# A selective scan on VectorE: two scans of 256 columns joined into one of 512, with the carry moved into the input

## What is computed

```python
def step(h, inp):
    dt_t, Bt, Ct, xt = inp
    dA = jnp.exp(dt_t[..., None] * A)
    h = dA * h + (xt * dt_t)[..., None] * Bt[:, None, :]
    y = jnp.einsum('bdn,bn->bd', h, Ct)
    return (h, y)
h0 = jnp.zeros((B, D_INNER, D_STATE), x.dtype)
_, ys = jax.lax.scan(step, h0, inputs)
y = jnp.transpose(ys, (1, 0, 2)) + x_ssm * D_param
```

## Time and profile before

| | us |
|---|---|
| median of 3 runs | 2015.43 |
| lowest, highest | 2011.38, 2016.09 |
| the profiled execution | 2016.48 |
| its span | 2014.4 |
| mean granted TensorE clock | 0.908 of full speed |

### The profile page before, as it was taken

How to read it: one execution, slowest core, us unless ns; L and a number is a source line. 1 busy time by engine, 2 the same in 40 slices (tenths; PEclk the granted TensorE clock), 3 DMA queues, 4 the chain that set the end, 5 groups by cost and what they waited for, 6 DMA issues and landing times. The chain is left out here.

```text
span 2014.4 us, 26268 instructions
## 1 busy us (share of the span) xinstructions
PE 1643.1 (82%) x7600; PEld 1165.7 (58%) x7600; DVE 1562.5 (78%) x2994; ACT 1021.0 (51%) x2232; POOL 919.6 (46%) x722
## 2 busy tenths in 40 slices
PE   5788777887878877778567999989997999989890
PEld 3566566666666666666454554753566454753570
DVE  1899999999999999999965435882578545881478
ACT  2766777667877577776632232415233232424240
POOL 0677787777777777767751010160105210260004
PEclk8888888988889888989768999989999999999995
DMA  3301111011111011110103000001000100000000
GB/s 122 136 18 48 59 59 54 11 55 58 59 59 44 17 58 58 59 48 6 57 12 111 0 22 0 1 1 46 21 1 0 47 21 0 1 0 21 0 1 21
DMA packets 38440, 71.25 MB, mean 35 GB/s; under 512 B 3698, under 2 KB 31955, under 8 KB 33971
## 3 DMA queue, kind: packets, MB, share of 16 engines
q1 hardware_dynamic: 38290, 69.45, 10.1%
HBM read 60.79 MB, written 8.65 MB: 34 GB/s over the span
## 5 line engine op out<-in xcount | busy, mean ns | idle before, releaser
L605 POOL TENSOR_TENSOR state_c<-state,c_bc 128x1024 f32<-128x1024 f32 x256 | 603.5, 2362 | 234.4 <-DVE state L668 220.9
L668 DVE TENSOR_TENSOR_SCAN state<-decay,carry,bu_ps 128x256 f32<-128x256 f32 x768 | 527.5, 727 | 0.0
L485 ACT ACTIVATE decay<-dt_sb,negA 128x256 f32<-128x256 f32 x1024 | 433.7, 498 | 3.1 <-issue 3.1
L653 DVE TENSOR_TENSOR bu_ps<-u_sb,b_ps 128x512 f32<-128x512 f32 x512 | 344.7, 673 | 47.7 <-POOL u_sb L546 40.1
L350 PE MATMUL y_ps<-ident_sb,state_c 128*128 128x128 f32 x2048 | 304.8, 298 | 23.0 <-DVE yg L636 13.9
L350 PEld LDWEIGHTS y_ps<-ident_sb,state_c 128*128 128x128 f32 x2048 | 263.8, 155 | 54.6 <-POOL state_c L605 27.3
L1225 POOL TENSOR_TENSOR big<-big,g_sb 128x1024 f32<-128x1024 f32 x29 | 68.7, 2369 | 453.0 <-DVE big L1333 432.1
L271 PE MATMUL w_ps<-xT_sb,w_conv 128*128 128x256 f32 (+1 forms) x1024 | 236.8, 385 | 13.8 <-DVE w_conv L706 12.8
L271 PEld LDWEIGHTS w_ps<-xT_sb,w_conv 128*128 128x128 f32 x1024 | 192.8, 193 | 40.0 <-DVE w_conv L706 12.8
L946 PE MATMUL ps<-kTm,qT 128*128 128x308 f32 x512 | 140.7, 438 | 29.9 <-DVE oT L1302 25.2
L668 DVE TENSOR_TENSOR_SCAN state<-decay,bu_ps 128x256 f32<-128x256 f32 x256 | 160.2, 665 | 0.0
(11 more groups left out here) (168 smaller groups left out, 2471.3 us busy)
## 6 DMA issues: line engine op xcount, KB each, us to landing
c_bc<-c_scratch SPq DMA_DIRECT2D x32, 1024.0 KB, 5.8
res<-in_x SPq DMA_DIRECT2D x16, 256.0 KB, 2.8
x_scratch<-res SPq DMA_DIRECT2D x16, 256.0 KB, 7.4
big<-x_scratch SPq DMA_DIRECT2D x4, 1024.0 KB, 7.5
xa<-x_scratch SPq DMA_DIRECT2D x4, 1024.0 KB, 5.7
out_x<-acc SPq DMA_DIRECT2D x4, 1024.0 KB, 4.8
xT_sb<-in_xT SPq DMA_DIRECT2D x12, 259.0 KB, 3.0
w_sb<-in_w SPq DMA_DIRECT2D x2, 1024.0 KB, 13.4
```

What stands on the lines that cost most here:

```text
L485: nc.scalar.activation(decay[:, n % RING, j, :], dt_sb[:, i[1] % 2, j, :], ACT.Exp, scale=negA[:, j * NS + n:j * NS + n + 1]).then_inc(s_d ...
L605: nc.gpsimd.tensor_tensor(state_c[:, n % RING, :, :], state[:, n % RING, :, :], c_bc[:, q, n, :].unsqueeze(1).to_broadcast([P, CT, TC]), A ...
L653: nc.vector.tensor_tensor(bu_ps[m % 3][:, :].rearrange("p (j n) -> p j n", j=2), u_sb[:, i[1] % 2, 2 * h:2 * h + 2, :], b_ps[n % 2][:, 0:T ...
L668: nc.vector.tensor_tensor_scan(state[:, n % RING, j, :], decay[:, n % RING, j, :], bu_ps[m % 3][:, e * TC:(e + 1) * TC], carry[:, n, j:j + ...
```

## The change

Two scans of a half step become one scan of 512 columns that runs over both tiles. For this to be right at the seam and at the start, column 0 of every `decay` tile is 0 (a memset of POOL at the start; ACT's exponentials now write columns 1 to 255 only), and the scan's initial value is always 0.0. What the first column should have got from the chunk before enters through u*b: column 0 of `bu_ps` becomes u*b + dA*carry. For this there are new instructions, in the chunks with c != 0:

- POOL `first_arg`: dt of the first column times A, for all states and tiles, 128x64, after `make_dt` at place 11.
- ACT `first_decay`: exp of it, 128x64, behind `take_y_back` at place 15, behind all decays of the turn. (These two are made for every chunk.)
- POOL `injections`: `inject` = first_dA * carry, 128x48 for the states 0 to 11 at place 13 of the turn before, and 128x16 for the states 12 to 15 at place 4 of the chunk's own turn.
- DVE, in each `make_bu`: the product leaves out column 0 (128x510), and a SCALAR_TENSOR_TENSOR of 128x2 writes column 0 of both tiles, with `b_ps[:, 0:1]` as its scalar (a pointer into PSUM). For the first half step it waits on `s_inj`, the first `injections`.

The scans no longer wait on `s_carry`, and for one `s_decay` in place of two.

```diff
@@ PE b_row
-                pe.wait_ge(s_bu, at(i, 2 * NS, 2 * n + 2))
+                pe.wait_ge(s_bu, at(i, 4 * NS, 4 * n + 4))
@@ ACT
+            def first_decay(k):
+                act.wait_ge(s_arg, at(k, 1, 1))
+                nc.scalar.activation(first_dA[:, k[1] % 2, :, :], first_dA[:, k[1] % 2, :, :], ACT.Exp).then_inc(s_dA, 1)
@@ ACT step
-                        act.wait_ge(s_scan, at(i, NS * CT, n * CT + CT))
+                        act.wait_ge(s_scan, at(i, 2 * NS, 2 * n + 2))
...
-                    nc.scalar.activation(decay[:, n % RING, j, :], dt_sb[:, i[1] % 2, j, :], ACT.Exp,
+                    nc.scalar.activation(decay[:, n % RING, j, 1:], dt_sb[:, i[1] % 2, j, 1:], ACT.Exp,
@@ ACT turn
+                if prepare:
+                    work.append((15, lambda: first_decay(k)))
@@ POOL
+            def first_arg(k):
+                q = k[1] % 2
+                if is_first(k):
+                    pool.wait_ge(s_par, 2)
+                pool.wait_ge(s_dt, at(k, 1, 1))
+                nc.gpsimd.tensor_tensor(first_dA[:, q, :, :], dt_sb[:, q, :, 0].unsqueeze(1).to_broadcast([P, NS, CT]),
+                                        negA[:, :].rearrange("p (j n) -> p n j", n=NS), ALU.mult).then_inc(s_arg, 1)
+
+            def injections(k, first, last):
+                if k[1] % CPB == 0:
+                    pool.sem_inc(s_inj, 1)
+                    return
+                if first == 0:
+                    pool.wait_ge(s_dA, at(k, 1, 1))
+                pool.wait_ge(s_carry, at(k, NS, last - NS))
+                nc.gpsimd.tensor_tensor(inject[:, first:last, :], first_dA[:, k[1] % 2, first:last, :],
+                                        carry[:, first:last, :], ALU.mult).then_inc(s_inj, 1)
@@ POOL turn
-                             (12, lambda: make_u(k))]
+                             (11, lambda: first_arg(k)), (12, lambda: make_u(k)),
+                             (13, lambda: injections(k, 0, NS - RING))]
+                work.append((4, lambda: injections(i, NS - RING, NS)))
@@ DVE make_bu
-                nc.vector.tensor_tensor(bu_ps[m % 3][:, :].rearrange("p (j n) -> p j n", j=2),
-                                        u_sb[:, i[1] % 2, 2 * h:2 * h + 2, :],
-                                        b_ps[n % 2][:, 0:TC].unsqueeze(1).to_broadcast([P, 2, TC]),
-                                        ALU.mult).then_inc(s_bu, 1)
+                c = 1 if i[1] % CPB else 0
+                nc.vector.tensor_tensor(bu_ps[m % 3][:, :].rearrange("p (j n) -> p j n", j=2)[:, :, c:],
+                                        u_sb[:, i[1] % 2, 2 * h:2 * h + 2, c:],
+                                        b_ps[n % 2][:, c:TC].unsqueeze(1).to_broadcast([P, 2, TC - c]),
+                                        ALU.mult).then_inc(s_bu, 1 if c else 2)
+                if c:
+                    if m == 0:
+                        dve.wait_ge(s_inj, at(i, 2, 1))
+                    elif m == 2 * (NS - RING):
+                        dve.wait_ge(s_inj, at(i, 2, 2))
+                    nc.vector.scalar_tensor_tensor(out=bu_ps[m % 3][:, :].rearrange("p (j n) -> p j n", j=2)[:, :, 0],
+                                                   in0=u_sb[:, i[1] % 2, 2 * h:2 * h + 2, 0],
+                                                   scalar=b_ps[n % 2][:, 0:1], in1=inject[:, n, 2 * h:2 * h + 2],
+                                                   op0=ALU.mult, op1=ALU.add).then_inc(s_bu, 1)
@@ DVE scans
-                    if c:
-                        dve.wait_ge(s_carry, at(i, NS, n + 1 - NS))
-                dve.wait_ge(s_bu, at(i, 2 * NS, 4 + m + 1))
-                for e in range(2):
-                    j = 2 * h + e
-                    dve.wait_ge(s_decay, at(i, NS * CT, n * CT + j + 1))
-                    nc.vector.tensor_tensor_scan(state[:, n % RING, j, :], decay[:, n % RING, j, :],
-                                                 bu_ps[m % 3][:, e * TC:(e + 1) * TC],
-                                                 carry[:, n, j:j + 1] if c else 0.0, ALU.mult, ALU.add).then_inc(s_scan, 1)
+                dve.wait_ge(s_bu, at(i, 4 * NS, 8 + 2 * m + 2))
+                dve.wait_ge(s_decay, at(i, NS * CT, n * CT + 2 * h + 2))
+                pair = slice(2 * h, 2 * h + 2)
+                nc.vector.tensor_tensor_scan(state[:, n % RING, pair, :].rearrange("p j n -> p (j n)"),
+                                             decay[:, n % RING, pair, :].rearrange("p j n -> p (j n)"),
+                                             bu_ps[m % 3][:, :], 0.0, ALU.mult, ALU.add).then_inc(s_scan, 1)
```

More of the change, by code:

```diff
@@ L82, in mamba_block @@
         carry = sb("carry", [P, NS, CT])
+        first_dA = sb("first_dA", [P, 2, NS, CT])
+        inject = sb("inject", [P, NS, CT])
         rest = sb("rest", [PARTS * BC, TC])
@@ L145, in mamba_block @@
         s_carry = sem("s_carry")
+        s_arg = sem("s_arg")
+        s_dA = sem("s_dA")
+        s_inj = sem("s_inj")
+        s_zero = sem("s_zero")
         s_sc = sem("s_sc")
@@ L506, in turn @@
                             what()
-            act.sem_inc(s_scan, RING * CT)
+            act.sem_inc(s_scan, RING * 2)
+            act.wait_ge(s_zero, 1)
             act.sem_inc(s_y, 32)
@@ L522, in _ @@
             next_lead(first)
+            first_decay(first)
             act.wait_ge(s_par, 2)
@@ L602, in turn @@
                         pool.wait_ge(s_cb[q][n // (NS // 2)], loads(i))
-                    pool.wait_ge(s_scan, at(i, NS * CT, (RING + n + 1) * CT))
+                    pool.wait_ge(s_scan, at(i, 2 * NS, (RING + n + 1) * 2))
                     pool.wait_ge(s_sum, at(i, NS, n + 1))
@@ L610, in turn @@
                             what()
+            nc.gpsimd.memset(decay[:, :, :, 0], 0.0).then_inc(s_zero, 1)
             for c, value in enumerate((0.5, 1.5, 1.0 / DM, LN_EPS, -0.5)):
@@ L622, in _ @@
             make_u(first)
+            first_arg(first)
+            injections(first, 0, NS - RING)
             turns(pool, turn)
@@ L650, in make_bu @@
                     dve.wait_ge(s_b, at(i, NS, n + 1))
-                dve.wait_ge(s_scan, at(i, NS * CT, RING * CT + 2 * (m - (1 if m < 2 else 2))))
-                nc.vector.tensor_tensor(bu_ps[m % 3][:, :].rearrange("p (j n) -> p j n", j=2),
-                                        u_sb[:, i[1] % 2, 2 * h:2 * h + 2, :],
-                                        b_ps[n % 2][:, 0:TC].unsqueeze(1).to_broadcast([P, 2, TC]),
-                                        ALU.mult).then_inc(s_bu, 1)
+                dve.wait_ge(s_scan, at(i, 2 * NS, RING * 2 + m - (1 if m < 2 else 2)))
@@ L658, in scans @@
             def scans(i, n, h):
-                m, c = 2 * n + h, i[1] % CPB
+                m = 2 * n + h
                 if h == 0:
                     dve.wait_ge(s_sc, at(i, NS, n + 1))
-                    if c:
-                        dve.wait_ge(s_carry, at(i, NS, n + 1 - NS))
-                dve.wait_ge(s_bu, at(i, 2 * NS, 4 + m + 1))
-                for e in range(2):
-                    j = 2 * h + e
-                    dve.wait_ge(s_decay, at(i, NS * CT, n * CT + j + 1))
-                    nc.vector.tensor_tensor_scan(state[:, n % RING, j, :], decay[:, n % RING, j, :],
-                                                 bu_ps[m % 3][:, e * TC:(e + 1) * TC],
-                                                 carry[:, n, j:j + 1] if c else 0.0, ALU.mult, ALU.add).then_inc(s_scan, 1)
+                dve.wait_ge(s_bu, at(i, 4 * NS, 8 + 2 * m + 2))
@@ L700, in turn @@
                     step(i, n, prepare, between)
-            dve.sem_inc(s_bu, 4)
+            dve.sem_inc(s_bu, 8)
             dve.sem_inc(s_sc, RING)
```

## The result

The changed kernel takes 2366.84 us (median of 4 runs, 2366.68 to 2368.79) against 2014.47 us before (4 runs, 2011.38 to 2016.09). The ratio is 1.176, with a 95% interval of 1.1745 to 1.1775: 352 us slower. The prediction was 2012 us, in a range of 1992 to 2028. It was wrong by far, and on the wrong side.

A forecast was written before the change was run, and what follows sets the result against it. DVE was taken to bound the kernel until 1060 us; of its 22.9 us saving, 19 are lost at the wait for `inject`, leaving -3.4 us: 2013.1 on the profiled execution, 2012 us predicted, range 1992 to 2028.

The forecast's parts named there:

- the price of the 128x2: DVE's new two-column instruction in each half step with carry: 0.13 us start to start, bounds 0.08 and 0.20.
- another page: Skill page "VectorE: DVE Perf Modes": a fixed term per instruction would make the half-step saving nil, sum near +4 us.
- The 128x2 is dear: Rival: DVE's 128x2, on the product's PSUM bank with a PSUM scalar, costs 0.20; +17 us, 2032 us; chance 0.12.
- scan of 512 columns, start to start: DVE's joined scan: 1.07 for the columns plus 0.05 fixed time, 1.12 us.
- half step with carry: DVE's product, 128x2 and scan: 0.58 + 0.13 + 1.12 = 1.83 us in place of 1.87, saving 0.043.
- what `first_arg` adds on POOL, start to start: POOL's 64-column instruction at the turn's end: 0.27 us, by a line between two and 256 columns.
- DVE's wait for `inject`, all turns: Idle before the 128x2 at 12 turn ends: 2.5 to 3 us in four, up to 2 in two, about 0.5 in six.
- sum against before: Turn-end changes, full savings in four chunks and the start add to -3.4 us; 19 of 22.9 us lost at the wait.
- the chain: PE, ACT, POOL work of fixed length from seven half steps into a turn to inject; only the first seven savings count.
- the case's own range: Range of the likeliest case, where the turn-end wait takes most of DVE's saving: 2004 to 2019 us; chance 0.45.
- little idle time before the 128x2: Sign against the forecast: no DVE idle time before the 128x2 would mean the gain shows, toward 1993 us.
- the pace: Sign: DVE's start-to-start time per half step inside a chunk with carry is 1.83 us; otherwise the prediction is wrong.

The follow-up runs named there:

- the run with one SBUF input: The changed kernel with the 128x2's added operand read from b_ps in PSUM in place of inject in SBUF, carry left out: 2017.88 us, ratio 1.0023.

## Why the prediction was wrong

**The step that failed** is the price of the 128x2, "I take 0.13, because L1419 is the same kind with the same kind of scalar", with its bounds of 0.08 and 0.20. From its own start to the start of the scan the stalled one takes 1.94 us (503.24 to 505.18), ten times the upper bound. The price of the instruction was right: 0.13 in the run with one SBUF input and 0.133 in the kernel before. What was missed is that it is the only one in the loop whose two tensor operands both lie in SBUF, and that POOL, all of whose inputs here lie in SBUF, is busy beside it for more than half of the time (113.73 of the 200 us from 400 to 600). L1419 too has two SBUF inputs, but in the stretch that was read, 1274.87 to 1286.76, POOL ran nothing at all. An instruction was priced by its kind and size, and not by what runs beside it.

**The trace of before had it.** DVE's L1245 adds two views of `stats`, both in SBUF. In the kernel before there are eight of 128x8. Five of them take 0.17 us and three 6.17; this is the first of the three:

```profile
1203.65 6.17 DVE L1245 TENSOR_TENSOR mean<-stats 128x8 f32<-128x8 f32 x1
```

POOL's timeline there:

```profile
1202.78 7.01 POOL L1221 TENSOR_TENSOR oT<-zero 128x4096 f32<-128x4096 f32 x1 [129.94 <-PE ps L999]
```

1203.65 + 6.17 = 1209.82, and POOL ends at 1209.79. The other two end beside a POOL L1221 in the same way. A small instruction that is 36 times as long as its twins is a bound from above for a small instruction, and it belonged into the range.

The Trainium skill has the rule, on the page "SBUF — State Buffer", in the section "Who interferes with whom": a DVE instruction with two SBUF inputs contends with a GpSimd instruction that reads SBUF, and whoever is first holds the shared ports for the whole instruction while the other is blocked. The trace agrees in what the runs vary: two SBUF inputs against one and a PSUM operand (1151 and 224 ns), and a shorter wait behind shorter POOL instructions (503 ns in place of 1151). It goes beyond that in one point: a wait of 5.83 us ran through three POOL instructions. That POOL, when it is second, waits for DVE was not tried. The prediction weighed another page and passed this one by.

**Two SBUF inputs are not the only case.** L1333 is a TENSOR_SCALAR with one tensor input in SBUF and two pointer scalars. With POOL idle it takes 0.40 us. Beside POOL it can be longer, up to 2.59 us. In the kernel before:

```profile
1298.64 2.45 DVE L1333 TENSOR_SCALAR big<-big,mean,scale 128x256 f32<-128x256 f32 x1
```

```profile
1298.48 2.46 POOL L1225 TENSOR_TENSOR big<-big,g_sb 128x1024 f32<-128x1024 f32 x1 [88.69 <-DVE big L1333]
```

It ends at 1301.09, POOL at 1300.94. No run varied this instruction, so its cause is open.

**The rivals.** "The 128x2 is dear" named the right instruction with a wrong reason (the PSUM bank, the pointer) and a price of 0.20. At 0.20 it came to 17 us over the kernel before, 2032 us, and could not reach 2367.

**What else the prediction said** can be read in the run with one SBUF input, which is the changed kernel without the stall:

| step | predicted | measured |
|---|---|---|
| scan of 512 columns, start to start | 1.12 | 1.13 |
| 128x2, start to start | 0.13 | 0.13 |
| half step with carry | 1.83 | 1.84 |
| what `first_arg` adds on POOL, start to start | 0.27 | 0.48 |
| DVE's wait for `inject`, all turns | about 18 | 13.0 |
| sum against before | -3.4 | +4.3 |

The half step took 1.84, so its saving was 0.035 and not 0.043. `first_arg`, priced on a line between plain operands, costs more on the chain. POOL's timeline in this run:

```profile
408.99 2.35 POOL L555 TENSOR_TENSOR dt_sb<-dt_sb,relu 128x1024 f32<-128x1024 f32 x1
411.43 0.42 POOL L567 TENSOR_TENSOR first_dA<-dt_sb,negA 128x64 f32<-128x64 f32 x1
411.79 2.37 POOL L639 TENSOR_TENSOR state_c<-state,c_bc 128x1024 f32<-128x1024 f32 x1
```

`state_c` stands 411.79 - 408.99 = 2.80 behind the start of `make_dt`, where it stood 412.10 - 409.78 = 2.32 behind it before. Of the 0.48, 0.36 is `first_arg` itself, and 0.12 is that it starts 2.44 behind `make_dt`, for whose end it waits. By an estimate from these numbers, the shorter saving and `first_arg` account for 8 x 7 and 4 x 32 half steps of 0.008, 1.5 us, and 12 x 0.21 = 2.5 us of the 7.7 that the sum is off; the other 3.7 us were not traced. The waits for `inject` were smaller and more even than forecast: 11 of them, the longest 1.9 us, and none of 2.5 to 3. The total of 2018 us lies inside the case's own range of 2004 to 2019. That the chain, and not DVE, sets the turn's length was right: moving one small POOL instruction ahead of two large ones gave 15.7 us.

In the changed kernel itself the wait for `inject` is only 6.4 us, in four turns, since the stalled DVE comes to it later. The prediction had it that little idle time before the 128x2 would come with a gain; here it came with a loss. Of its signs the pace was the one that told: 3.65 and 1.84 us in turn (502.66, 506.31, 508.15) in place of 1.83. PE's granted clock fell along, from 0.908 to 0.841 of full speed, with a PE that pauses more (422.6 us before the matmuls of `b_row`). With DVE's stall removed by one operand it is 0.908 again.

## What to carry to other kernels

Before adding a VectorE instruction to a loop that GpSimd shares, count its tensor inputs that lie in SBUF. With two of them its price is not its own length but at least what is left of the GpSimd instruction that runs beside it, and the profile shows this as busy time and not as a wait. Put one operand into PSUM (here: add in place to what the product left there), or make the GpSimd instructions short; and price a new instruction by the slowest of its like in the trace, not only by the mean of the nearest.

## What was not expected of the hardware

- A DVE instruction of two columns was 2.0 us long beside a POOL instruction of 2.35 us and 0.22 us without it; 2308 ns was the longest of 384, 214 the shortest.
- With POOL busy without a pause, a DVE instruction of two columns lasted 5.83 us, through three POOL instructions; in other places DVE got in between two of them.
- Cutting the POOL instruction into four made the kernel 247 us faster, though POOL's step grew from 2.35 to 2.79 us.
- An add in place of 128x2 in PSUM behind a scan takes 0.05 us from start to start, less than half of the 0.13 of the product with a pointer scalar. The two differ in place, kind and scalar, and no run separates these.
